# The gated output bias of the first attention: added to the residual by GpSimd, four tiles at a time, or by a TensorE product of ones and three bf16 parts

## The chip, the cores and the metric

One core of one Trainium2 chip runs the whole program. Times are device microseconds (us) of that core; lower is better. The engines are called by the names that the profile has for them: PE is TensorE (PEld its weight loads), DVE VectorE, ACT ScalarE, POOL GpSimd, SP SyncE.

## What is computed

Two layers work on 8192 tokens of 128 numbers (128 sequences of 64). The change lies in the first step of the first layer, an attention over a context, whose result is gated and added to x:

```python
def _L0_xattn_ref(q_in, k_in, v_in, mask, Wq, bq, Wk, bk, Wv, bv, Wo, bo):
    q = _split_heads(q_in @ Wq + bq)              # 16 heads of 8
    k = _split_heads(k_in @ Wk + bk)
    v = _split_heads(v_in @ Wv + bv)
    logits = jnp.einsum('bhqd,bhkd->bhqk', q, k) / jnp.sqrt(jnp.asarray(D_QKV, jnp.float32))
    w = jax.nn.softmax(logits - mask * FMAX, axis=-1)
    o = jnp.einsum('bhqk,bhkd->bhqd', w, v)
    return o.transpose(0, 2, 1, 3).reshape(...) @ Wo + bo

x = x + jnp.tanh(g_xattn[0]) * _L0_xattn_ref(_layernorm(x, axis=-1), ctx_1024, ctx_1024, mask, ...)
x = x + jnp.tanh(g_ffn[0]) * _L0_ffn_ref(_layernorm(x, axis=-1), ...)    # 8 experts, top 2
x = x + jnp.tanh(g_xattn[1]) * _L1_xattn_ref(_layernorm(x, axis=-1), ctx_1024, ctx_1024, mask_BxS2_bk1, ...)
x = x + jnp.tanh(g_ffn[1]) * _L1_ffn_ref(_layernorm(x, axis=-1), ...)
```

With the gate written as g = tanh(g_xattn[0]), the first line adds o @ (g Wo) + g bo to x. It is where g bo is added that differs.

## The kernel before

x lies in SBUF for the whole run, as 64 tiles of 128 tokens by 128 numbers (`x_sb`). The first attention runs over these tiles in 64 steps plus three that drain it; t is the step, s = t // 4 the quad (four tiles, `QUAD`), j = t % 4 the place in it. Each engine has its own queue, written out by hand in the order of the steps, and waits on semaphores. The routing of the tokens to experts (logits, first and second choice, places, scattering of rows by indirect DMA) is woven into the same steps some tiles later, and so are the keys and values of the second attention.

What a step t holds, for each engine, in the order of its queue:

- PE: scores of two tiles (even j, L798); `heads_product(t)`: 32 small products of probabilities and values for tile t-3 (L897), and behind them, for tile t-4, the output product into `turn`, a strip of the PSUM bank `ps_o` (L903 and L904), whose end is told by `o_ps`; `probs_transposes(t)` of tile t-2 (L913, waits for POOL's `shifted`); some projections; `heads_transpose(t)` (L922), which writes `turn` again and so waits for DVE's `y_sb` (the residual has been read out) and `o_sb`.
- DVE: scores minus mask (L1390); `reciprocals` (L1363) and `head_sums` (L1367), which wait for `o_ps`; `residual(t)` (L1373), x_sb plus `turn` for tile t-4; `x_stats` (L1377); routing steps, above all `places(c)` at j = 2 of every even s from 4 on (L1208 to L1217); and the row maximum `top` (L1425), the last large thing of the step.
- POOL: scores minus `top` in place (L500, semaphore `shifted`), then at some steps small things, and from step 18 on two indirect DMAs that scatter rows (`send_rows`, L481). At j = 0 it also takes the powers of the second layernorm (L454, L456).
- ACT: exponentials of the transposed scores (L618), the copy of the heads (L622), normalised x and others.

The gated bias `bo` (scaled by tanh at L398) is put into PSUM by PE: `bias_parts()` on POOL splits it once, at t = 1, into three bf16 parts in rows 0, 32 and 64 of `bias_row` (`bias_step` counts to 9), and in each of the 64 steps a product of `ones_row` and `bias_row` starts the accumulation in `turn` (L903) that the fp32 product of heads and `wo` ends (L904).

Of the kernel before, what the change touches and what calls it, by code (L numbers as in the profile page):

```python
# [5 lines left out]
ALU = mybir.AluOpType  # L6
ACT = mybir.ActivationFunctionType
AX_X = mybir.AxisListType.X
F32 = mybir.dt.float32
F32R = mybir.dt.float32r  # L10
BF16 = mybir.dt.bfloat16
# [3 lines left out]
P = 128  # L15
BATCH, SEQ, DM = 128, 64, 128
NTOK = BATCH * SEQ
TILES = NTOK // P
QUAD = 4
# [39 lines left out]
def layer0_and_experts(nc, ctx, d, g, sb, sem):  # L59

    x_sb, stats, ident, tg = g["x_sb"], g["stats"], g["ident"], g["tanh_gates"]
# [4 lines left out]
    wq, wk, wv, wo, bv, bo = (sb(f"a_{n}", [P, DM], F32) for n in ("wq", "wk", "wv", "wo", "bv", "bo"))  # L66
    bq, bk = (sb(f"a_{n}", [P, 1], F32) for n in ("bq", "bk"))
    mask = sb("a_mask", [P, SEQ], F32)
    with ExitStack() as until_routed:
        def first(name, shape, dt):  # L70
# [21 lines left out]
    xn_t, ctx_t, heads_t = g["keys0"], g["values0"], g["wq1"]  # L92
# [6 lines left out]
    probs_t = sb("a_probs_t", [P, 2, GROUPS, P], F32)  # L99
    rsum = sb("a_rsum", [P, HEADS], F32)  # L100
    heads = sb("a_heads", [P, HEADS, DH], F32)
    bias_hi, bias_mid, bias_row, ones_row = (sb(f"a_{n}", [65, P], BF16) for n in ("bias_hi", "bias_mid", "bias_row", "ones_row"))
    bias_rest = sb("a_bias_rest", [65, P], F32)

    TE = [P, CT, EXPERTS]
    rw = sb("r_rw", [EXPERTS, DM], F32)
# [47 lines left out]
    (gates_in, q_in, k_in, v_in, mask_in, wo_in, ident_step, gates_ready, bq_set, own_set, stats1, step1, var_ready,  # L154
     rstd_ready, nmr_ready, vals_set, ones_set, mask_set, bo_set, xn_ready, xt_ps, ct_ps, xt_sb, ct_sb, q_ps,
     k_ps, q_sb, k_sb, v_ps, v_sb, s_ps, s_sb, top_ready, shifted, pt_ps, pt_sb, o_ps, rsum_ready, o_sb, ot_ps, ot_sb,
     y_sb, stats2, bias_step) = (sem("a_" + n) for n in (
         "gates_in", "q_in", "k_in", "v_in", "mask_in", "wo_in", "ident_step", "gates_ready", "bq_set", "own_set", "stats1", "step1",
         "var_ready", "rstd_ready", "nmr_ready", "vals_set", "ones_set", "mask_set", "bo_set", "xn_ready",
         "xt_ps", "ct_ps", "xt_sb", "ct_sb", "q_ps", "k_ps", "q_sb", "k_sb", "v_ps", "v_sb", "s_ps", "s_sb",  # L160
         "top_ready", "shifted", "pt_ps", "pt_sb", "o_ps", "rsum_ready", "o_sb", "ot_ps", "ot_sb", "y_sb", "stats2", "bias_step"))
    (rw_in, bias_in, consts, const_step, resets_set, mv_ready, var2_ready, rstd2_ready, nmr2_ready, row_ready, x2t_ps, x2t_sb, l_ps,
     l_sb, small_ps, small_sb, hi_done, lo_done, weights_out, first_pick, second_pick, ratio_ready, cn_ps, placed, gate_set,
     ids, ends_ready, table_step, tables_ready, padded) = (sem("r_" + n) for n in (
# [25 lines left out]
    turn = ps_o[:, TURN_AT:TURN_AT + P]  # L190
# [177 lines left out]
    def _(pool):  # L368
# [30 lines left out]
        pool.tensor_scalar(wo[:], wo[:], tg[:, 0:1], None, ALU.mult).then_inc(bo_set, 1)  # L399
        pool.wait_ge(bo_set, 2)  # L400

        def bias_parts():
            pool.memset(ones_row[:], 1.0).then_inc(bias_step, 1)
            pool.memset(bias_row[:], 0.0).then_inc(bias_step, 1)
            pool.tensor_copy(bias_hi[:], bo[0:65]).then_inc(bias_step, 1)
            pool.wait_ge(bias_step, 3)
            pool.tensor_tensor(bias_rest[:], bo[0:65], bias_hi[:], ALU.subtract).then_inc(bias_step, 1)
            pool.wait_ge(bias_step, 4)
            pool.tensor_copy(bias_mid[:], bias_rest[:]).then_inc(bias_step, 1)
            pool.wait_ge(bias_step, 5)  # L410
            pool.tensor_tensor(bias_rest[:], bias_rest[:], bias_mid[:], ALU.subtract).then_inc(bias_step, 1)
            pool.wait_ge(bias_step, 6)
            pool.tensor_copy(bias_row[0:1], bias_hi[0:1]).then_inc(bias_step, 1)
            pool.wait_ge(bias_step, 7)
            pool.tensor_copy(bias_row[32:33], bias_mid[32:33]).then_inc(bias_step, 1)
            pool.wait_ge(bias_step, 8)
            pool.tensor_copy(bias_row[64:65], bias_rest[64:65]).then_inc(bias_step, 1)
            pool.wait_ge(bias_step, 9)

        def routing_consts(nth):  # L420

# [73 lines left out]
        for s in range(SUPERS):  # L495
            for j in range(QUAD):
                t = s * QUAD + j
                m = s - 2
                pool.wait_ge(top_ready, t + 1)
                pool.tensor_tensor(probs[:, j], probs[:, j], top[:, j].unsqueeze(2).broadcast_to([P, HEADS, SEQ]),  # L500
                                   ALU.subtract).then_inc(shifted, 1)
                if j == 0 and m >= 0:
                    powers(m)
                if t == 1:
                    bias_parts()
                r = 2 + s
                if j == 2 and there(r, len(ROUNDS)):
                    pool.wait_ge(var_ready, r + 1)
                    scale(ROUNDS[r][0] // QUAD)
                if j == 3 and there(r, len(ROUNDS)):  # L510
                    for n in range(ROUNDS[r][0] // QUAD + 1, ROUNDS[r][1] // QUAD):
                        scale(n)
                if s == 1:
                    routing_consts(j)
                c = s // 2 - 1
                if j == 0 and s % 2 == 0 and RING <= c < NCH:
                    renumber(c)
                if t >= SCATTER_LAG:
                    send_rows(t - SCATTER_LAG)
# [271 lines left out]
    def _(pe):  # L791
# [97 lines left out]
        def heads_product(t):  # L889
            j = t % QUAD  # L890
# [8 lines left out]
                                       vals[(t - 3) // QUAD % 2][:, (j + 1) % 4, b, cols], start=True, stop=True)  # L899
            if there(t - 4, TILES):  # L900
                if t == 4:
                    pe.wait_ge(bias_step, 9)
                pe.matmul(turn, ones_row[:], bias_row[:], start=True, stop=False)  # L903
                mm = pe.matmul(turn, heads_t[:], wo[:], start=False, stop=True)  # L904
            mm.then_inc(o_ps, 1)

        def probs_transposes(t):
# [22 lines left out]
        for s in range(SUPERS):  # L930
            n, u, m = s + 1, s % 2, s - 2
            for j in range(QUAD):
                t = s * QUAD + j
# [190 lines left out]
    def _(dve):  # L1124
# [244 lines left out]

        def residual(t):  # L1370
            dve.wait_ge(o_ps, t - 2)
            xs = x_sb[:, t - 4]
            dve.tensor_tensor(xs, xs, turn, ALU.add).then_inc(y_sb, 1)  # L1373

# [1015 lines left out]
```

## Time and profile before

| | |
|---|---|
| median of 3 runs | 895.19 us (894.82 to 900.1) |
| span of the profiled execution | 960.7 us |
| busy in it: PE, DVE, ACT, POOL | 746.5, 742.0, 612.7, 594.2 us |
| first attention | from about 15 us to about 415 us of the span |

The profiled execution was 65 us longer than the median of the runs that were timed. A row of the timeline gives the start, the duration, the engine, the line, the operation, what is written from what is read, and how many instructions were put together; in brackets stands the idle time before it and who ended it. In a row of waits stand the waiting engine and line, the releaser, the total in us, the number of waits and the longest. Ends of matmuls are modelled, so that starts on PE are the better measure of its pace.

### The profile page before, as it was taken

The numbers are of one execution on the slowest core, as the hardware profiler recorded it, in microseconds if no ns is written. First come the engines' busy times: TensorE is split into PE (matmuls) and PEld (weight loads), VectorE is DVE, ScalarE is ACT, GpSimd is POOL, SyncE is SP. The second block draws the span as 40 slices with busy tenths as digits, with TensorE's granted clock in tenths as the row PEclk, the third lists the DMA queues.
The fourth block names the chain that finished last, engine by engine and source line by source line (L and its number), as shares of the span: only waits on it lengthen the run. The fifth ranks groups of instructions, "written<-read, shape, count | busy, mean of one in ns | idle before, by whom it ended". The sixth has DMA issues, their size and how long they took to land. (4 is left out here: it accounts for less than half of the span.)

```text
span 960.7 us, 19492 instructions
## 1 busy us (share of the span) xinstructions
PE 746.5 (78%) x6609; PEld 573.8 (60%) x6612; DVE 742.0 (77%) x1800; ACT 612.7 (64%) x1222; POOL 594.2 (62%) x571
## 2 busy tenths in 40 slices
PE   4898788988888888788698888999963889256255
PEld 2666577666666667666576766777751667122144
DVE  5999987877777887568566666777844799799998
ACT  5666556757576664567366656666753878399493
POOL 4675377777777777564556566665665983388600
PEclk9999989999999999899798999999985999676556
DMA  9327222222223123646476566575627832000023
GB/s 246 101 78 128 86 73 101 82 101 78 100 80 111 47 93 123 214 140 204 150 260 217 193 239 216 208 259 202 222 93 239 273 110 78 14 0 1 0 66 111
DMA packets 88625, 128.20 MB, mean 133 GB/s; under 512 B 19392, under 2 KB 62352, under 8 KB 82512
## 3 DMA queue, kind: packets, MB, share of 16 engines
q1 hardware_dynamic: 78528, 107.63, 34.6%
q0 software_dynamic: 9120, 18.91, 5.6%
q8 instruction: 54, 0.88, 0.4%
q10 hardware_dynamic: 880, 0.43, 0.2%
q14 instruction: 43, 0.35, 0.1%
HBM read 82.66 MB, written 44.18 MB: 132 GB/s over the span
## 5 line engine op out<-in xcount | busy, mean ns | idle before, releaser
L491 POOL DMA_INDIRECT m_results<-a_probs,e_to x156 | 161.6, 1036 | 94.5 <-issue 50.2
L500 POOL TENSOR_TENSOR a_probs<-a_probs,a_top 128x1024 f32<-128x1024 f32 x64 | 122.0, 1907 | 91.5 <-DVE a_top L1425 90.6
L481 POOL DMA_INDIRECT m_tokens_to<-r_rows,r_place x128 | 131.3, 1026 | 53.3 <-issue 31.0
L710 ACT ACTIVATE room<-a_ps_s,e_bias 128x512 f32<-128x512 f32 x156 | 107.3, 697 | 79.5 <-PE a_ps_s L1007 64.6
L1452 DVE CAST e_hp<-room 128x512 fp32r<-128x512 f32 x156 | 70.1, 449 | 82.8 <-ACT room L710 30.9
L618 ACT ACTIVATE a_probs_t<-a_ps_pt 128x512 f32<-128x512 f32 x128 | 70.1, 592 | 94.3 <-PE a_ps_pt L913 91.2
L1454 DVE TENSOR_TENSOR e_hp<-room,e_hp 128x512 fp32r<-128x512 f32 x156 | 109.9, 705 | 5.4
L1390 DVE TENSOR_TENSOR a_probs<-a_ps_s,a_mask 128x1024 f32<-128x1024 f32 x64 | 77.9, 1217 | 16.0 <-PE a_ps_s L798 11.5
L897 PEld LDWEIGHTS a_ps_o<-a_vals,a_probs_t 128*64 128x64 f32 x2048 | 68.1, 140 | 26.0 <-issue 25.2
L897 PE MATMUL a_ps_o<-a_vals,a_probs_t 128*64 128x18 f32 x2048 | 75.7, 214 | 4.8 <-issue 4.6
L1425 DVE TENSOR_REDUCE a_top<-a_probs 128x16 f32<-128x1024 f32 x64 | 77.2, 1206 | 0.2
L913 PE MATMUL a_ps_pt<-ident,a_probs 128*128 128x128 f32 x512 | 73.5, 291 | 1.5 <-DVE n_values L1287 1.2
L1003 PE MATMUL a_ps_s<-e_xt,e_weights 128*128 128x512 f32 x156 | 68.2, 437 | 8.2 <-issue 5.1
L2219 DVE TENSOR_REDUCE d_hpeak<-d_hid 128x1 f32<-128x2048 f32 (+1 forms) x36 | 70.6, 2043 | 3.4 <-ACT d_hid L2116 3.4
L913 PEld LDWEIGHTS a_ps_pt<-ident,a_probs 128*128 128x128 f32 x512 | 63.7, 151 | 2.9 <-DVE n_values L1287 2.4
L1007 PE MATMUL a_ps_s<-e_xt,e_weights 128*128 128x512 f32 x156 | 62.6, 401 | 0.0
L1004 PE MATMUL a_ps_s<-e_xt,e_weights 128*128 128x512 f32 x156 | 62.5, 401 | 0.0
L1014 PE MATMUL a_ps_pt<-e_hp,e_weights 128*128 128x512 f32 x100 | 41.5, 415 | 12.1 <-ACT room L722 7.9
L1363 DVE RECIPROCAL a_rsum<-a_ps_o 128x16 f32<-128x16 f32 x64 | 16.1, 251 | 41.5 <-PE a_ps_o L904 23.3
L729 ACT ACTIVATE a_probs<-a_ps_pt,room 128x128 f32<-128x128 f32 x156 | 44.2, 373 | 3.1 <-PE a_ps_pt L1032 3.1
L922 PE MATMUL a_ps_o<-ident,a_heads 128*128 128x128 f32 x64 | 20.8, 325 | 32.1 <-DVE x_sb L1373 30.1
L553 ACT ACTIVATE room<-a_ps,a_own_bk,a_own 128x512 f32<-128x512 f32 x64 | 44.6, 783 | 1.8 <-PE a_ps L818 1.8
(334 smaller groups left out, 2012.9 us busy)
## 6 DMA issues: line engine op xcount, KB each, us to landing
e_weights<-m_weights_to SPq DMA_DIRECT2D x39, 1024.0 KB
room<-m_tokens_to SPq DMA_DIRECT2D x39, 264.0 KB
m_weights_to<-r_parts SPq DMA_DIRECT2D x8, 1024.0 KB
c_two<-m_results SPq DMA_DIRECT2D x3, 1536.0 KB, 11.8
a_ctx_in<-in_ctx_dram SPq DMA_DIRECT2D x17, 256.0 KB, 3.5
m_keys_t<-n_keys SPq DMA_DIRECT2D x16, 256.0 KB
m_values<-n_values SPq DMA_DIRECT2D x16, 256.0 KB
out_dram<-x_sb SPq DMA_DIRECT2D x15, 256.0 KB, 2.3
```

The source lines that it names most:

```text
L481: pool.indirect_dma_start(tokens_to, bass.IndirectOffsetOnAxis(ap=place[:, k, q:q + 1], axis=0), rows[:, c % RING, q % CT, k, :], None).th ...
L491: pool.indirect_dma_start(results, bass.IndirectOffsetOnAxis(ap=to[:, v, r:r + 1], axis=0), y[:, v, r], None).then_inc(returned[v], 16)
L500: pool.tensor_tensor(probs[:, j], probs[:, j], top[:, j].unsqueeze(2).broadcast_to([P, HEADS, SEQ]), ALU.subtract).then_inc(shifted, 1)
L618: act.activation(probs_t[:, j % 2, 4 * h:4 * h + 4, :], ps_pt[h][:], ACT.Exp).then_inc(pt_sb, 1)
L710: act.activation(h[:, c], ps_h[c], ACT.Gelu_apprx_tanh, bias=bias[:, n % ROWS, c:c + 1]).then_inc(h_sb, 1)
L897: mm = pe.matmul(ps_o[SEQ * b:SEQ * b + SEQ, cols], probs_t[:, (j + 1) % 2, gr, SEQ * b:SEQ * b + SEQ], vals[(t - 3) // QUAD % 2][:, (j + ...
L913: mm = pe.transpose(ps_pt[h][:, k, :], probs[:, (t + 2) % 4, 8 * h + 2 * k:8 * h + 2 * k + 2] .rearrange("p j k -> p (j k)"), ident[:])
L1390: dve.tensor_tensor(probs[:, j].rearrange("p (i k) q -> p i k q", i=BANDS), ps_s[:, :, j % 2], mask[:].unsqueeze(1).unsqueeze(1).broadcast ...
L1425: dve.tensor_reduce(top[:, j], probs[:, j], AX_X, ALU.max).then_inc(top_ready, 1)
L1452: dve.tensor_copy(hp[:, c, 0], h[:, c]).then_inc(h_hi, 1)
L1454: dve.tensor_tensor(hp[:, c, 1], h[:, c], hp[:, c, 0].bitcast(F32), ALU.subtract).then_inc(h_lo, 1)
L2219: dve.tensor_reduce(hpeak[:, e, column:column + 1], h, AX_X, op).then_inc(hpeak_ready, 1)
```

## The change

POOL no longer splits the bias. In its place, at j = 1 of each of the 16 quads and right behind that step's subtraction, it adds `bo` to the quad's four tiles of `x_sb` in one 128x512 instruction (`add_bias`). It waits for `xn_ready`, that is until ACT has normalised these four tiles, since the layernorm must see x without the bias. PE's product of ones and bias parts goes away, in all 64 steps; the output product starts its own accumulation, and at t = 4 waits for the gated `wo` (`bo_set`) in place of the nine steps of the split. DVE's residual waits for `bias_added` of its quad as well. Five small tiles in SBUF go away.

```diff
@@ gpsimd
-        def bias_parts():
-            pool.memset(ones_row[:], 1.0).then_inc(bias_step, 1)
-            pool.memset(bias_row[:], 0.0).then_inc(bias_step, 1)
-            pool.tensor_copy(bias_hi[:], bo[0:65]).then_inc(bias_step, 1)
...
-            pool.tensor_copy(bias_row[64:65], bias_rest[64:65]).then_inc(bias_step, 1)
-            pool.wait_ge(bias_step, 9)
+        def add_bias(n):
+            four = slice(QUAD * n, QUAD * n + QUAD)
+            pool.wait_ge(xn_ready, QUAD * n + QUAD)
+            pool.tensor_tensor(x_sb[:, four], x_sb[:, four], bo[:].unsqueeze(1).broadcast_to([P, QUAD, DM]), ALU.add)\
+                .then_inc(bias_added, 1)
...
-                if t == 1:
-                    bias_parts()
+                if j == 1:
+                    add_bias(s)
@@ tensor
                 if t == 4:
-                    pe.wait_ge(bias_step, 9)
-                pe.matmul(turn, ones_row[:], bias_row[:], start=True, stop=False)
-                mm = pe.matmul(turn, heads_t[:], wo[:], start=False, stop=True)
+                    pe.wait_ge(bo_set, 2)
+                mm = pe.matmul(turn, heads_t[:], wo[:], start=True, stop=True)
@@ vector
         def residual(t):
             dve.wait_ge(o_ps, t - 2)
+            dve.wait_ge(bias_added, (t - 4) // QUAD + 1)
             xs = x_sb[:, t - 4]
             dve.tensor_tensor(xs, xs, turn, ALU.add).then_inc(y_sb, 1)
```

The order of PE's instructions in one step of the first attention before (L897 the heads, L903 the bias, L904 the output product, L913 the transposes of the scores, L922 the transpose of the heads):

```order
L897 MATMUL a_ps_o<-a_vals,a_probs_t 64x18 [waits a_v_sb,a_y_sb,a_pt_sb,a_ot_sb,a_o_sb]
L897 MATMUL a_ps_o<-a_vals,a_probs_t 64x18 x15
L903 MATMUL a_ps_o<-a_bias_row,a_ones_row 128x128
L904 MATMUL a_ps_o<-a_wo,wq 128x128
L913 MATMUL a_ps_pt<-ident,a_probs 128x128 [waits a_pt_sb,a_shifted,a_xt_sb]
L913 MATMUL a_ps_pt<-ident,a_probs 128x128 x7
```

The same of a step in the changed kernel, where the lines are L883, L889, L898 and L907:

```order
L883 MATMUL a_ps_o<-a_vals,a_probs_t 64x18 [waits a_v_sb,a_y_sb,a_pt_sb,a_ot_sb,a_o_sb]
L883 MATMUL a_ps_o<-a_vals,a_probs_t 64x18 x15
L889 MATMUL a_ps_o<-a_wo,wq 128x128
L898 MATMUL a_ps_pt<-ident,a_probs 128x128 [waits a_pt_sb,a_shifted,n_v1_raw]
L898 MATMUL a_ps_pt<-ident,a_probs 128x128 x7
L907 MATMUL a_ps_o<-ident,a_heads 128x128 [waits a_o_sb,a_y_sb]
```

The one bf16 product between the heads and the output product is gone, and nothing else has moved on PE.

The order of POOL's instructions at the last quad of the changed kernel (L486 is the subtraction that was L500, L440 and L442 are the powers, L467 the scatter that was L481):

```order
L486 TENSOR_TENSOR a_probs<-a_probs,a_top 128x1024 [waits a_top_ready]
L440 TENSOR_TENSOR r_rstd<-r_mv,r_power 128x4 [waits r_mv_ready]
L442 TENSOR_TENSOR r_rstd<-r_rstd,r_power 128x4 [waits r_var2_ready]
L467 DMA m_tokens_to<-r_rows,r_place 73216x132 x2
L486 TENSOR_TENSOR a_probs<-a_probs,a_top 128x1024 [waits a_top_ready]
L403 TENSOR_TENSOR x_sb<-x_sb,a_bo 128x512 [waits a_xn_ready]
L467 DMA m_tokens_to<-r_rows,r_place 73216x132 x2
L486 TENSOR_TENSOR a_probs<-a_probs,a_top 128x1024 [waits a_top_ready]
```

L403 is the new instruction: behind the subtraction of j = 1 and ahead of that step's two scatters; before, the scatters followed at once.

## Rows read from the trace of the kernel before

**Rows 1.** Busy time by stage: span, then PE, PEld, DVE, ACT, POOL, clock, DMA
```profile
15.00:400.00 385.00, 326.70 (x4429) 255.79 (x4428) 315.85 (x841) 236.07 (x475) 261.30 (x232) 0.96 0.34 106
```

**Rows 2.** Waits between 60 and 400 us: total, times, longest
```profile
POOL a_probs L500 <- DVE a_top L1425: 78.9, 28, 4.7
...
PE a_ps_o L922 <- DVE x_sb L1373: 25.5, 27, 2.3
DVE a_rsum L1363 <- PE a_ps_o L904: 23.3, 18, 2.8
```

**Rows 3.** All instructions of line L903: min/median/max ns, first and last start
```profile
L903 PE MATMUL a_ps_o<-a_bias_row,a_ones_row x64: 229/230/289, 34.5 to 413.2; 65*128 65x128 bf16 x64
```

**Rows 4.** Timeline of PE and DVE, steps 39 and 41
```profile
240.54 0.23 PE L903 MATMUL a_ps_o<-a_bias_row,a_ones_row 65*128 65x128 bf16 x1
240.60 0.44 PE L904 MATMUL a_ps_o<-a_wo,wq 128*128 128x128 f32 x2
240.88 1.04 PE L913 MATMUL a_ps_pt<-ident,a_probs 128*128 128x128 f32 x8
...
241.13 0.26 DVE L1363 RECIPROCAL a_rsum<-a_ps_o 128x16 f32<-128x16 f32 x1 [1.23 <-PE a_ps_o L904]
...
253.11 1.04 PE L913 MATMUL a_ps_pt<-ident,a_probs 128*128 128x128 f32 x8
```

**Rows 5.** POOL's groups of instructions: count, busy us, mean ns, idle before
```profile
L2072 POOL TENSOR_TENSOR x_sb<-x_sb,room 128x512 f32<-128x512 f32 x16 | 20.0, 1271 | 0.0
...
L2059 POOL TENSOR_TENSOR room<-x_sb,mean 128x512 f32<-128x512 f32 x16 | 16.8, 1051 | 25.4 <-DVE ext L2190 24.4 <-DVE room L2211 0.9
```

**Rows 6.** Timeline of POOL, the first and last of the nine split instructions
```profile
24.33 0.20 POOL L403 MEMSET a_ones_row<- 65x128 bf16 x1
...
27.03 0.29 POOL L417 CAST a_bias_row<-a_bias_rest 1x128 bf16<-1x128 f32 x1
```

**Rows 7.** Timeline of POOL, a quad of odd s (steps 37 to 40)
```profile
236.11 1.91 POOL L500 TENSOR_TENSOR a_probs<-a_probs,a_top 128x1024 f32<-128x1024 f32 x1
...
244.81 1.92 POOL L500 TENSOR_TENSOR a_probs<-a_probs,a_top 128x1024 f32<-128x1024 f32 x1
...
253.50 1.90 POOL L500 TENSOR_TENSOR a_probs<-a_probs,a_top 128x1024 f32<-128x1024 f32 x1 [4.37 <-DVE a_top L1425]
```

**Rows 8.** Timeline, DVE's variances beside and without POOL's subtraction
```profile
27.88 1.90 POOL L500 TENSOR_TENSOR a_probs<-a_probs,a_top 128x1024 f32<-128x1024 f32 x1 [0.56 <-DVE a_top L1425]
...
28.54 1.27 DVE L1136 TENSOR_TENSOR mean<-stats 128x12 f32<-128x12 f32 x1
...
49.94 0.18 DVE L1136 TENSOR_TENSOR mean<-stats 128x12 f32<-128x12 f32 x1
```

**Rows 9.** Timeline of POOL and DVE, a quad of even s (s = 14)
```profile
354.45 1.92 POOL L500 TENSOR_TENSOR a_probs<-a_probs,a_top 128x1024 f32<-128x1024 f32 x1
...
357.03 0.29 DVE L1208 TENSOR_TENSOR_SCAN r_upto<-r_resets,r_total 128x72 f32<-128x72 f32 x1
...
360.35 1.90 POOL L500 TENSOR_TENSOR a_probs<-a_probs,a_top 128x1024 f32<-128x1024 f32 x1 [1.49 <-DVE a_top L1425]
```

**Rows 10.** Timeline of POOL, DVE and PE, s = 13 (steps 53 to 55)
```profile
332.01 1.91 POOL L500 TENSOR_TENSOR a_probs<-a_probs,a_top 128x1024 f32<-128x1024 f32 x1
...
334.00 0.27 DVE L1315 TENSOR_TENSOR r_past<-r_tnum,r_tile_end 128x104 f32<-128x104 f32 x1
...
338.42 0.28 DVE L1373 TENSOR_TENSOR x_sb<-x_sb,a_ps_o 128x128 f32<-128x128 f32 x1
...
338.75 0.33 PE L922 MATMUL a_ps_o<-ident,a_heads 128*128 128x128 f32 x1
```

**Rows 11.** Timeline of DVE and PE, the residual and L922 in step 59
```profile
362.15 0.28 DVE L1373 TENSOR_TENSOR x_sb<-x_sb,a_ps_o 128x128 f32<-128x128 f32 x1
...
363.22 0.27 PE L922 MATMUL a_ps_o<-ident,a_heads 128*128 128x128 f32 x1
```

**Rows 12.** Timeline of POOL, its first wait behind the last quad
```profile
396.27 0.19 POOL L454 TENSOR_TENSOR r_rstd<-r_mv,r_power 128x4 f32<-128x4 f32 x1 [5.05 <-DVE r_mv L1357]
```

More of the change, by code:

```diff
@@ L101, in layer0_and_experts @@
     heads = sb("a_heads", [P, HEADS, DH], F32)
-    bias_hi, bias_mid, bias_row, ones_row = (sb(f"a_{n}", [65, P], BF16) for n in ("bias_hi", "bias_mid", "bias_row", "ones_row"))
-    bias_rest = sb("a_bias_rest", [65, P], F32)
     TE = [P, CT, EXPERTS]
@@ L156, in layer0_and_experts @@
      k_ps, q_sb, k_sb, v_ps, v_sb, s_ps, s_sb, top_ready, shifted, pt_ps, pt_sb, o_ps, rsum_ready, o_sb, ot_ps, ot_sb,
-     y_sb, stats2, bias_step) = (sem("a_" + n) for n in (
+     y_sb, stats2, bias_added) = (sem("a_" + n) for n in (
          "gates_in", "q_in", "k_in", "v_in", "mask_in", "wo_in", "ident_step", "gates_ready", "bq_set", "own_set", "stats1", "step1",
@@ L160, in layer0_and_experts @@
          "xt_ps", "ct_ps", "xt_sb", "ct_sb", "q_ps", "k_ps", "q_sb", "k_sb", "v_ps", "v_sb", "s_ps", "s_sb",
-         "top_ready", "shifted", "pt_ps", "pt_sb", "o_ps", "rsum_ready", "o_sb", "ot_ps", "ot_sb", "y_sb", "stats2", "bias_step"))
+         "top_ready", "shifted", "pt_ps", "pt_sb", "o_ps", "rsum_ready", "o_sb", "ot_ps", "ot_sb", "y_sb", "stats2", "bias_added"))
     (rw_in, bias_in, consts, const_step, resets_set, mv_ready, var2_ready, rstd2_ready, nmr2_ready, row_ready, x2t_ps, x2t_sb, l_ps,
@@ L400, in _ @@
         pool.wait_ge(bo_set, 2)
-        def bias_parts():
-            pool.memset(ones_row[:], 1.0).then_inc(bias_step, 1)
-            pool.memset(bias_row[:], 0.0).then_inc(bias_step, 1)
-            pool.tensor_copy(bias_hi[:], bo[0:65]).then_inc(bias_step, 1)
[L406 to L416, printed above, removed]
-            pool.tensor_copy(bias_row[64:65], bias_rest[64:65]).then_inc(bias_step, 1)
-            pool.wait_ge(bias_step, 9)
+        def add_bias(n):
[3 more added lines that the diff above has]
+                .then_inc(bias_added, 1)
         def routing_consts(nth):
```

## The prediction

> **What bounds the kernel now.** I read the busy time by stage first. Over the first attention PE is busy 326.7 of 385.0 us, DVE 315.9, POOL 261.3, ACT 236.1, with the clock at 0.96 of the higher level (2.4 GHz) [rows 1]. No engine is full, so the 64 steps (385.0 / 64 = 6.0 us each) are set by a ring of waits, and the waits come next. Between 60 and 400 us, 57 steps, PE waits 27 times for DVE's residual before it may transpose the heads, DVE waits 18 times for the output product, and POOL waits 28 times, 78.9 us in all, for DVE's row maximum [rows 2]. So the ring runs PE, DVE, PE: heads and output product, reciprocal to residual, transpose of the heads. POOL hangs on it as a side branch with time to spare. The change takes a little from PE inside the ring and puts more on POOL beside it. The reader should ask three things: how wide PE's slot is, whether POOL can take the addition, and whom a longer POOL disturbs.
>
> **PE, 64 bf16 products removed.** One lasts 0.230 us by its own row [rows 3]. That is not what it costs, since matmuls overlap: in the timeline L903 starts at 240.54 and L904 at 240.60 [rows 4]. The 64 distances from L903 to L904 lie between 0.06 and 0.08 us, so I take 0.065: 64 x 0.065 = 4.2 us of PE's time. It shortens the run only where the ring passes through PE. For the floor I count the steps in which DVE waits for the output: 18 of 57 [rows 2], so 4.2 x 18 / 57 = 1.3 us. For the ceiling I take every step, 4.2. Beside those 18 there are steps in which PE goes into L922 without any wait (about 57 - 27 = 30, partly the same ones), where PE itself is the pace. I choose 40 slots of 64, between the two ends: **-2.6 us**.
>
> **POOL, the split removed, 16 additions put in.** The split ran from 24.33 to 27.32, 3.0 us once [rows 6]. It was wanted by PE at step 4, at 34.5 us [rows 3], so it cost nothing and its going gives nothing. For an addition the trace has the same shape in the last stage: 128x512, x_sb plus a bias repeated four times, 1.271 us; the nearest cheaper row, where the second input is one number for each tile, is 1.051 [rows 5]. I take 1.27; between 1.05 and 1.27 the total is 16.8 to 20.3 us. Who covers it: POOL's steps of a quad are a subtraction of 1.9 us each and two scatters ((244.81 - 236.11) / 2 = 4.35 us from one subtraction to the next [rows 7], so some 2.45 for the two), and the tightest place is a quad of odd s. There the three subtractions from j = 1 on run back to back with the scatters, the first at 236.11 and the last at 244.81, and then POOL idles 4.37 us until DVE's maximum releases it at 253.50 [rows 7]. The addition comes behind the first of these and moves the other two by 1.27. The last of them would end at 246.73 + 1.27 = 248.00, while PE transposes that tile at 253.11 [rows 4], 5.1 us later. The subtraction of j = 1 itself, which has the least room (ended 238.02, used by PE at 240.88 [rows 4], 2.86 us), lies ahead of the addition and is not moved. In quads of even s POOL idles 1.49 us (s = 14) or more before the next subtraction and takes up the 1.27 there [rows 9]; only at s = 13 is the idle shorter, 0.59, and the rest of the 1.27 is then at most 0.7 us of lateness. Behind the last quad POOL idles 5.05 us until 396.27 [rows 12], so the scatters that follow are not pushed either. Term: **0**; without that cover it would be 20.3 - 3.0 = 17.3.
>
> **The new waits.** DVE's residual of quad n comes first in step 4n + 4; the addition was issued behind the subtraction of step 4n + 1, three steps of 6 us earlier. ACT has normalised quad n in the quad before, so POOL does not stand at `xn_ready`, with its scatters queued behind it. Both are 0.
>
> **DVE, held up by POOL's addition.** This is the term that speaks against the change. Beside POOL's subtraction a DVE instruction of 128x12 whose two inputs both lie in SBUF took 1.27 us, from 28.54 to the very end of the subtraction at 29.78, and 0.18 without it [rows 8]. DVE's large instructions of the stage (PSUM and one SBUF input, or one input) show no such stretch. So I looked which two-input instructions of DVE fall into the 1.27 us behind the subtraction of j = 1. Of `places`, L1208 starts at 357.03, 0.66 us behind the subtraction's end at 356.37 [rows 9], and would be held to 357.60. The same is seen in s = 6, 8, 10, 12 and 14, with distances of 0.79, 0.78, 0.91, 0.68 and 0.66 us, which makes 0.44 + 0.45 + 0.32 + 0.55 + 0.57 = 2.3 us. In s = 13 the table look-up starts at 334.00, just as the subtraction (332.01 + 1.91) is over [rows 10], and would lose 1.2 us. In the other ten quads nothing falls in. What of this reaches the ring is read one step later, where PE transposes the heads: in step 55 the residual ends at 338.70 and PE goes at 338.75, no room [rows 10]; in step 59 it ends at 362.43 and PE goes at 363.22, 0.7 us of room [rows 11]. Steps 35 and 43 look like 59, and steps 27 and 51 like 55. So s = 6, 12 and 13 pay, 0.44 + 0.55 + 1.15 = **+2.1 us**; bounds are 0 (DVE's wait of the next step takes it up) and 3.5.
>
> The Trainium skill, SBUF — State Buffer, section "Who interferes with whom", says that a DVE instruction with two SBUF inputs and a GpSimd one that reads SBUF lock each other out for the whole instruction; this trace agrees, 1.27 against 0.18 us. The Trainium skill's GPSIMD Engine Reference, section "Engine selection", advises VectorE for elementwise additions, and section "Elementwise — side-by-side cycle accounting" gives 4497 ns for 2048 numbers per partition, which makes an estimate of 1.12 us for 512 and 18.0 us for 16, where the row makes 20.3; POOL's idle time covers either.
>
> **The sum.** -2.6 + 0 + 2.1 = -0.5 us on a span of 960.7, so 960.2. The profiled execution is 65 us above the median of the timed runs, 895.19; carried over in proportion the change is again -0.5: 894.7.
>
> **Rivals.** (a) *Likeliest, 0.83:* slots gained and lock losses nearly cancel. With its bounds, -4.2 + 0 to -1.3 + 3.5 = +2.2, it gives 891 to 897.5. (b) *Slower by the lock, 0.06:* if the additions move relative to DVE's work so that a two-input instruction is held the whole 1.27 us in every quad and nothing takes it up, 16 x 1.27 - 4.2 = +16.1, 911.3. It decides (more than 9 us) from about 10 quads on; against it stand ten quads in which nothing falls into the window. (c) *Slower by POOL's load, 0.04:* in the timed runs the steps are shorter than 6.0 us, by the ratio of the times 5.6. If POOL's idle time is what shrank, the later subtractions reach PE late and up to 17.3 us come back, 912.5. Against it: 78.9 us of idle POOL over 57 steps, 1.4 us in each, 5.5 a quad, and 1.27 is needed. (d) *Faster, 0.07:* the bf16 product between fp32 ones costs its full 0.230 us, in every step: 64 x 0.23 = -14.7, 880.5. Against it is the 0.06 us between starts, and DVE's reciprocal at 241.13, 0.09 us behind the modelled end of the output product (240.60 + 0.44) [rows 4], so that PE's records hide no more time at that place.
>
> About 1% (9 us) is what can be told from no change for this kernel, since its own runs lie between 894.82 and 900.1. That gives faster 0.07, same 0.83, slower 0.10. The range must hold (a) and the scatter of the runs, of which one was 5 us above the median: 889 to 901.
>
> **What would show it.** In the changed profile: 64 fewer matmuls, with the first output matmul starting about 0.03 us behind the last one of the heads. 16 POOL additions of 1.27 us. The subtraction of odd quads' j = 2 starting some 3 us behind DVE's maximum, instead of 1.7, with no wait of PE for it. No wait of DVE's residual for POOL. L1208's successor lasting 0.6 to 0.9 us instead of 0.29 in five quads. The last step of the attention within 3 us of where it was (L903 last at 413.2 [rows 3]). A residual that waits for `bias_added`, PE waiting for `shifted`, or stretched DVE instructions in most quads would make it wrong.

## The result, and the profile after

The changed kernel takes **911.76 us** (median of 4, 910.37 to 918.22) beside 896.28 us (median of 4, 894.82 to 900.1) of the kernel before: ratio 1.0169, 95% interval 1.0117 to 1.022. It is 15 us slower. The forecast was 894.7, range 889 to 901, with 0.10 for slower.

The profiled execution of the changed kernel (busy us, share of its span, instructions):

```profile
span 907.4 us, 19437 instructions
...
PE 732.0 (81%) x6548; PEld 560.3 (62%) x6548; DVE 755.6 (83%) x1800; ACT 618.6 (68%) x1222; POOL 608.9 (67%) x578
```

This span is 53 us *below* the 960.7 of the trace that the prediction was read from, although the kernel is slower. The two profiled executions cannot be compared as they are, and the experiments have to settle that first. Waits of the changed kernel between 60 and 400 us (total, times, longest):

```profile
POOL a_probs L486 <- DVE a_top L1411: 53.5, 29, 3.9
...
PE a_ps_o L907 <- DVE x_sb L1359: 27.4, 28, 2.3
DVE a_rsum L1348 <- PE a_ps_o L889: 26.6, 21, 4.4
```

POOL's wait for the row maximum fell from 78.9 to 53.5 us; the other two were 25.5 and 23.3 [rows 2] and seem hardly to have moved. Against a trace of the kernel before that belongs to the timed runs (below) the reading is another: POOL's wait was 57.9 there, and PE's for the residual 19.1. PE waits nowhere for `shifted`, no residual waits for POOL, the addition lasts 1.27 us as forecast. What is new stands where DVE's scan of `places` (L1193, before L1208) meets POOL, here in s = 8:

```profile
213.93 1.92 POOL L486 TENSOR_TENSOR a_probs<-a_probs,a_top 128x1024 f32<-128x1024 f32 x1
215.79 1.28 POOL L403 TENSOR_TENSOR x_sb<-x_sb,a_bo 128x512 f32<-128x512 f32 x1
...
215.95 1.30 DVE L1193 TENSOR_TENSOR_SCAN r_upto<-r_resets,r_total 128x72 f32<-128x72 f32 x1
```

In the trace before it lasted 0.29 us and began 0.66 us behind the subtraction's end in s = 14 [rows 9], 0.78 us in s = 8. Here, in s = 8, it begins 0.10 us behind it (215.85) and ends at 217.25, 0.18 us behind the end of the addition (217.07).

### The profile page after: what moved, and what is told of

Its sections match the earlier page's. It is cut to its first block and busy times, and to the rows that moved or that the text cites. A ratio compares the mean times of both kernels' runs of the same rounds, so it can differ in the third digit from the quotient of the medians.

```text
span 907.4 us, 19437 instructions
## 1 busy us (share of the span) xinstructions
PE 732.0 (81%) x6548; PEld 560.3 (62%) x6548; DVE 755.6 (83%) x1800; ACT 618.6 (68%) x1222; POOL 608.9 (67%) x578
## 5 line engine op out<-in xcount | busy, mean ns | idle before, releaser
L477 POOL DMA_INDIRECT m_results<-a_probs,e_to x156 | 158.1, 1014 | 58.7 <-issue 36.4
L486 POOL TENSOR_TENSOR a_probs<-a_probs,a_top 128x1024 f32<-128x1024 f32 x64 | 122.1, 1907 | 69.4 <-DVE a_top L1411 68.8
L467 POOL DMA_INDIRECT m_tokens_to<-r_rows,r_place x128 | 132.6, 1036 | 47.8 <-issue 31.2
L1438 DVE CAST e_hp<-room 128x512 fp32r<-128x512 f32 x156 | 73.1, 469 | 39.2 <-ACT room L696 34.5
L883 PEld LDWEIGHTS a_ps_o<-a_vals,a_probs_t 128*64 128x64 f32 x2048 | 66.7, 141 | 20.3 <-issue 19.7
L883 PE MATMUL a_ps_o<-a_vals,a_probs_t 128*64 128x18 f32 x2048 | 73.1, 214 | 0.3 <-ACT wq L608 0.3
L898 PE MATMUL a_ps_pt<-ident,a_probs 128*128 128x128 f32 x512 | 70.7, 284 | 1.5 <-DVE n_values L1272 1.5
L988 PE MATMUL a_ps_s<-e_xt,e_weights 128*128 128x512 f32 x156 | 66.5, 426 | 5.6 <-DMA e_weights<-m_weights_to 5.6
L898 PEld LDWEIGHTS a_ps_pt<-ident,a_probs 128*128 128x128 f32 x512 | 60.8, 147 | 3.2 <-DVE n_values L1272 2.0
L992 PE MATMUL a_ps_s<-e_xt,e_weights 128*128 128x512 f32 x156 | 61.4, 394 | 0.0
L989 PE MATMUL a_ps_s<-e_xt,e_weights 128*128 128x512 f32 x156 | 61.3, 393 | 0.0
L2102 ACT ACTIVATE d_hid<-d_ps_h,d_b,d_outscale 128x512 f32<-128x512 f32 x64 | 44.7, 788 | 1.5 <-PE d_ps_h L2143 1.5
L907 PE MATMUL a_ps_o<-ident,a_heads 128*128 128x128 f32 x64 | 20.7, 324 | 29.8 <-DVE x_sb L1359 28.8
L2143 PE MATMUL d_ps_h<-d_xqt,d_wqt 128*128 128x512 bf16 x64 | 26.8, 566 | 21.7 <-ACT d_xqt L2094 21.7
```

What stands on the lines that cost most here:

```text
L467: pool.indirect_dma_start(tokens_to, bass.IndirectOffsetOnAxis(ap=place[:, k, q:q + 1], axis=0), rows[:, c % RING, q % CT, k, :], None).th ...
L477: pool.indirect_dma_start(results, bass.IndirectOffsetOnAxis(ap=to[:, v, r:r + 1], axis=0), y[:, v, r], None).then_inc(returned[v], 16)
L883: mm = pe.matmul(ps_o[SEQ * b:SEQ * b + SEQ, cols], probs_t[:, (j + 1) % 2, gr, SEQ * b:SEQ * b + SEQ], vals[(t - 3) // QUAD % 2][:, (j + ...
L898: mm = pe.transpose(ps_pt[h][:, k, :], probs[:, (t + 2) % 4, 8 * h + 2 * k:8 * h + 2 * k + 2] .rearrange("p j k -> p (j k)"), ident[:])
L1438: dve.tensor_copy(hp[:, c, 0], h[:, c]).then_inc(h_hi, 1)
```

## Experiments

Every ratio is to the kernel before, timed beside it on the same chip. For the traces I use one measure, the distance from one row maximum of DVE (`top`) to the next, which is the length of a step of the first attention.

**The two kernels once more on one chip.** The same source as before and as after, no edit.

> The kernel before, profiled once more, because its profiled execution (960.7 us) lay 65 us above its timed runs while that of the changed kernel (907.4) did not. All theories: 895 to 900 us timed. If the first profile was a disturbed execution, this one's span is near 893, and the waits of the two attention traces can be compared; if profiling itself costs this kernel 65 us, the span is again near 960.

> The changed kernel, a second time and on the same chip as the others: 911 us if the 1.7 per cent hold on another chip, 896 if they were scatter.

On this chip the kernel before takes 960.07 us (median of 31, 948 to 971), 7% more than in the timing above. `base_again` measured 1.0015 (0.997 to 1.006), `after_again` 1.0057 (1.0004 to 1.011). The span of the first profile, 960.7, fits this chip's 960 and not the 895 that the prediction was to be made for. So the trace I had read was, as far as its numbers tell, of such a chip, on which this kernel runs slower (below: the slow chip). There the change costs little. The same two kernels on other chips:

> The changed kernel on whatever chip comes next. In the group before, all four kernels and the kernel before lay at 958 to 962 us, where the kernel before had 896 in the first comparison: chips differ by more than the change. Theory A (the loss of 15 us is real where the expert stage isn't slowed by its loads): 1.01 to 1.02 times the kernel before on a chip on which that takes 895 us, 1.00 on one where it takes 960. Theory C (the loss was the scatter of single executions, 948 to 971 for one kernel on one chip): 1.00 on both.

> The kernel before, for a trace from a chip on which it takes some 897 us: the first two traces of it are from chips on which it takes 960. On such a chip the distances between DVE's row maxima in steps 26, 34, 42, 50, 54 and 58 should be those of the kernel without the bias (6.0, 6.0, 6.3, 6.2, 5.9 and 6.2 us), and the 64 maxima take 344 us from first to last, 4 us less without PE's product if that product costs its slot.

On the first of them before took 897.82 us (median of 13) and the changed kernel 915.25 (median of only 4, 905.22 to 919.55): 1.0179 (1.0109 to 1.025). `base_fast`, the kernel before on a third chip, took 896.65 with a span of 894.8 (one run). This profile fits the timed runs; from here on it is the comparison. Its waits between 60 and 400 us:

```profile
POOL a_probs L500 <- DVE a_top L1425: 57.9, 29, 5.2
...
DVE a_rsum L1363 <- PE a_ps_o L904: 23.9, 20, 5.8
...
PE a_ps_o L922 <- DVE x_sb L1373: 19.1, 24, 2.1
```

Beside these, PE's wait for DVE's residual has grown from 19.1 to 27.4 us in the changed kernel. The loss stands in the ring itself, at the place where PE waits for DVE, and not at POOL.

What differs between the chips in the place in question: PE, DVE and POOL of the kernel before in the first trace, s = 8 (in brackets the idle time before):

```profile
209.64 0.91 PE L897 MATMUL a_ps_o<-a_vals,a_probs_t 128*64 128x18 f32 x15
210.96 0.31 PE L897 MATMUL a_ps_o<-a_vals,a_probs_t 128*64 128x18 f32 x4 [0.41 <-issue]
211.71 0.58 PE L897 MATMUL a_ps_o<-a_vals,a_probs_t 128*64 128x18 f32 x13 [0.44 <-issue]
...
211.28 1.91 POOL L500 TENSOR_TENSOR a_probs<-a_probs,a_top 128x1024 f32<-128x1024 f32 x1
...
211.81 1.22 DVE L1390 TENSOR_TENSOR a_probs<-a_ps_s,a_mask 128x1024 f32<-128x1024 f32 x1 [0.93 <-remote]
...
213.97 0.29 DVE L1208 TENSOR_TENSOR_SCAN r_upto<-r_resets,r_total 128x72 f32<-128x72 f32 x1
```

and the same stretch in `base_fast`:

```profile
208.13 1.11 PE L897 MATMUL a_ps_o<-a_vals,a_probs_t 128*64 128x18 f32 x32
...
209.29 1.21 DVE L1390 TENSOR_TENSOR a_probs<-a_ps_s,a_mask 128x1024 f32<-128x1024 f32 x1
...
209.77 1.91 POOL L500 TENSOR_TENSOR a_probs<-a_probs,a_top 128x1024 f32<-128x1024 f32 x1
...
211.38 0.47 DVE L1208 TENSOR_TENSOR_SCAN r_upto<-r_resets,r_total 128x72 f32<-128x72 f32 x1
211.88 0.17 DVE L1211 COPY r_total<-r_upto 128x8 f32<-128x8 f32 x1
```

On the slow chip both engines stand still for some 0.9 us ahead of the scan, which no engine of the core explains, so that DVE came to it 0.78 us *behind* the subtraction (211.28 + 1.91 = 213.19). (`base_again` shows the same: 0.87 us without work, then the scan 0.67 us behind the subtraction.) On the other chip they don't stand still, and DVE comes to it 0.30 us *before* the subtraction's end (211.68), and is already held: 0.47 us in place of 0.29, ending at 211.85. In s = 6, 10, 12 and 14 it comes 0.29 to 0.54 us before the end. An addition put right behind the subtraction then finds the scan waiting; only in s = 8, where the changed kernel's step 33 is longer, does it come 0.1 us behind the end.

**The product of ones and bias gone, nothing on POOL.** The changed kernel without the addition and without DVE's wait for it; the bias is left out of the result.

```diff
-                if j == 1:
-                    add_bias(s)
...
-            dve.wait_ge(bias_added, (t - 4) // QUAD + 1)
```

> The changed kernel without the 16 additions and without DVE's wait for them: the bias is left out of the computation. PE's product is gone, and nothing stands in its place. Theory A (POOL's additions cost the time, by DVE's lock or by POOL's load): 891 to 895 us, the -2.6 us of the forecast. Theory B (taking PE's product away costs it, by a lower clock or by a shifted order of waits): 908 to 912.

> The changed kernel without the additions (the bias is left out of the computation), beside it. Theory A with POOL's additions as the cause: 0.995 to 1.00 times the kernel before on a fast chip. Theory B (PE's missing product is the cause): as slow as the changed kernel. Theory C: 1.00 like all.

1.002 (0.9974 to 1.0067) on the slow chip, 1.0015 (0.9979 to 1.0052) on the other. Taking 64 products from PE gives back nothing that the timing can show, at most 0.2%. The trace says how little there is; PE in a step of `base_fast`:

```profile
278.05 1.11 PE L897 MATMUL a_ps_o<-a_vals,a_probs_t 128*64 128x18 f32 x32
279.10 0.23 PE L903 MATMUL a_ps_o<-a_bias_row,a_ones_row 65*128 65x128 bf16 x1
279.16 0.44 PE L904 MATMUL a_ps_o<-a_wo,wq 128*128 128x128 f32 x2
279.44 0.82 PE L913 MATMUL a_ps_pt<-ident,a_probs 128*128 128x128 f32 x6
```

and in one of the changed kernel (the trace shown first):

```profile
217.87 1.11 PE L883 MATMUL a_ps_o<-a_vals,a_probs_t 128*64 128x18 f32 x32
218.91 0.49 PE L889 MATMUL a_ps_o<-a_wo,wq 128*128 128x128 f32 x2
219.23 1.04 PE L898 MATMUL a_ps_pt<-ident,a_probs 128*128 128x128 f32 x8
```

From the start of the heads to the output product it is 1.11 us before and 1.04 after (medians over more than 50 steps each): the slot of 0.065 did go. But the output product then takes from its start to the transposes' 0.32 to 0.33 in place of 0.27 to 0.28, and from heads to transposes 1.37 stands against 1.39. What is left is 0.02 us a step, 1.3 us in 64. And since the output product's two passes now last 0.49 us and not 0.44, its modelled end moved from 1.55 to 1.53 us behind the heads' start, 0.02 again. Why the passes take longer the trace doesn't say.

**The addition alone, the product kept.** The kernel before with the 16 additions at the same place, counted on `bias_step`; the bias is added twice.

```diff
...
+                if j == 1:
+                    add_bias(s)
...
+            dve.wait_ge(bias_step, 9 + (t - 4) // QUAD + 1)
```

> The kernel before with the 16 additions put in beside PE's product, so that the bias is added twice. Theory A: 911 to 915 us, as slow as the changed kernel or 3 us slower. Theory B: 895 to 898, since PE has all its work still. If both are slow only together (neither this nor the run without bias is slow), the sum of small shifts is the cause.

> The kernel before with the 16 additions put in and PE's product kept (the bias is added twice), now with traces of both kinds of chip in mind: 1.015 to 1.02 on a chip where the kernel before takes 897 us, since the additions alone make the loss; 1.00 where it takes 960.

1.0029 (0.9984 to 1.0075) on the slow chip, 1.0161 (1.0109 to 1.0213) on another, against 1.017 to 1.018 for the changed kernel. Within the intervals the whole of the loss comes with the additions.

**The addition moved away from the scan.** At j = 2 from s = 5 on, behind another subtraction.

```diff
-                if j == 1:
+                if j == (1 if s < 5 else 2):
```

> The changed kernel with the additions of quads 5 to 15 behind the subtraction of j = 2 in place of j = 1, where DVE has no instruction with two SBUF inputs for the next 3 us. POOL's load is the same. Theory L (POOL's addition holds up DVE's scan, L1193, for its whole length in six quads and L1297 in one): the 1.2 us in steps 26, 34, 42, 50, 54 and 58 are gone, 1.003 to 1.008 times the kernel before where the changed one has 1.018. Theory P (POOL's 20 us of added load, whatever its place): 1.015 to 1.020.

1.0066 (1.0033 to 1.0099), 903.53 us beside the 912.38 of the kernel above on the same chip: more than half of the loss is gone, with as many additions of the same kind.

**The same time on POOL without reading SBUF.** In place of each addition, at its old place, three writes of zeros into an unused tile; the bias is left out.

```diff
-            pool.tensor_tensor(x_sb[:, four], x_sb[:, four], bo[:].unsqueeze(1).broadcast_to([P, QUAD, DM]), ALU.add)\
-                .then_inc(bias_added, 1)
+            for k in range(3):
+                if 3 * n + k:
+                    pool.wait_ge(bias_added, 3 * n + k)
+                pool.memset(dummy[:], 0.0).then_inc(bias_added, 1)
...
-            dve.wait_ge(bias_added, (t - 4) // QUAD + 1)
+            dve.wait_ge(bias_added, 3 * ((t - 4) // QUAD + 1))
```

> The changed kernel with three memsets of 128x380 in place of each addition, some 1.3 us of POOL at the same place that write SBUF and read nothing (the bias is left out of the computation). Theory L by reads: DVE's scan isn't held beyond the subtraction's end (0.5 us), and the time is that of the kernel without bias, 1.000 to 1.005. Theory P: 1.015 to 1.020, as the changed kernel. If the scan is held though nothing is read, the lock is of writes too, and the time is that of the changed kernel as well.

1.0066 (1.0036 to 1.0096), above the 1.000 to 1.005 that was expected if only reads hold DVE. POOL's group of these writes, and its timeline at s = 8 (the three writes as one row, then the second of them by itself):

```profile
L407 POOL MEMSET a_dummy<- 128x380 f32 x48 | 20.0, 417 | 1.8
```

```profile
205.85 1.92 POOL L489 TENSOR_TENSOR a_probs<-a_probs,a_top 128x1024 f32<-128x1024 f32 x1
207.69 1.38 POOL L407 MEMSET a_dummy<- 128x380 f32 x3
208.18 0.41 POOL L407 MEMSET a_dummy<- 128x380 f32 x1
...
207.86 0.29 DVE L1196 TENSOR_TENSOR_SCAN r_upto<-r_resets,r_total 128x72 f32<-128x72 f32 x1
208.19 0.44 DVE L1199 COPY r_total<-r_upto 128x8 f32<-128x8 f32 x1
```

POOL is as busy as with the additions (20.0 against 16 x 1.27 = 20.3 us) and at the same place, and the scan runs in 0.29 us beside it. In s = 6, 10, 12 and 14, where the subtraction already holds it, the scan is over 0.18 us behind the subtraction, while the writes go on. So it is the reading that holds the scan, not POOL's time. But the small copy behind the scan, which has one input, lasts 0.44 us in place of 0.17 and ends at 208.63, 0.04 us behind the second write: some instructions of DVE are held by writes. The scan over the whole run, minimum, median and maximum in ns, in `base_fast`, the changed kernel, the addition with the product kept, the later addition and the write-only one:

```profile
L1208 DVE TENSOR_TENSOR_SCAN r_upto<-r_resets,r_total x8: 287/470/719, 123.1 to 425.4; 128x72 f32<-128x72 f32 x8
```

```profile
L1193 DVE TENSOR_TENSOR_SCAN r_upto<-r_resets,r_total x8: 285/1496/1953, 120.9 to 435.1; 128x72 f32<-128x72 f32 x8
```

```profile
L1216 DVE TENSOR_TENSOR_SCAN r_upto<-r_resets,r_total x8: 291/1502/1945, 121.2 to 433.1; 128x72 f32<-128x72 f32 x8
```

```profile
L1193 DVE TENSOR_TENSOR_SCAN r_upto<-r_resets,r_total x8: 287/392/735, 118.9 to 427.3; 128x72 f32<-128x72 f32 x8
```

```profile
L1196 DVE TENSOR_TENSOR_SCAN r_upto<-r_resets,r_total x8: 287/390/727, 119.3 to 423.7; 128x72 f32<-128x72 f32 x8
```

The Trainium skill, SBUF — State Buffer, section "Who interferes with whom", states just this border: a DVE instruction with two SBUF inputs contends with a GpSimd one that reads SBUF, not with one that only writes it. By that rule, the traces agree: 1.30 us beside the addition, 0.29 beside the writes.

**A version without either loss.** The additions spread by hand to steps in which neither a scan nor the layernorm's powers stand behind them (for s from 6 on mostly steps of the quads of odd s).

```diff
+        ADDS = {1: (0,), 4: (1,), 9: (2,), 13: (3,), 17: (4,), 22: (5,), 23: (6,), 30: (7,), 31: (8,), 38: (9,), 39: (10,),
+                46: (11,), 47: (12,), 55: (13, 14), 62: (15,)}
...
-                if j == 1:
-                    add_bias(s)
+                for n in ADDS.get(t, ()):
+                    add_bias(n)
```

> The changed kernel with every addition in a step where POOL has idle time and DVE no two-input instruction behind POOL's subtraction: steps 1, 4, 9, 13, 17, and from quad 5 on two additions in each odd quad (steps 22 and 23, 30 and 31, 38 and 39, 46 and 47, both 13 and 14 in step 55, 15 in step 62). Theory L with the rest of the loss (1.007 of the later placing against 1.0015 without bias) made of POOL's powers coming late to DVE and ACT in quads 1, 13 and 15: 1.000 to 1.004 times the kernel before. If the rest is POOL's load wherever it stands: 1.006 to 1.010. A gain over the kernel before isn't expected by either, since PE's product gave back nothing. On a chip where the kernel before takes 960 us: 1.00 by both.

900.75 us beside 898.49, 1.0031 (1.0006 to 1.0057). This is the change nearly without its cost, and it still isn't faster than the kernel before, as the 1.0015 without any addition already says: no run shows a gain on PE.

**The steps side by side.** Length of a step in us (from one row maximum to the next), all on the chips where the kernel before takes some 897 us; below, all 63 of them.

| step | before (`base_fast`) | no addition | later | write only | product kept | spread | after |
|---|---|---|---|---|---|---|---|
| 26 (s = 6, scan) | 6.02 | 6.03 | 6.03 | 6.06 | 7.24 | 6.03 | 7.23 |
| 34 (s = 8, scan) | 6.02 | 6.03 | 5.84 | 6.02 | 6.88 | 5.84 | 6.85 |
| 42 (s = 10, scan) | 6.27 | 6.29 | 6.29 | 6.32 | 7.50 | 6.28 | 7.50 |
| 50 (s = 12, scan) | 6.19 | 6.22 | 6.21 | 6.24 | 7.43 | 6.19 | 7.42 |
| 54 (s = 13, scan of the tiles' ends) | 5.93 | 5.94 | 5.95 | 5.89 | 7.16 | 5.94 | 7.16 |
| 58 (s = 14, scan) | 6.21 | 6.21 | 6.21 | 6.24 | 7.44 | 6.21 | 7.42 |
| 33 | 4.89 | 4.90 | 5.20 | 5.20 | 5.19 | 5.20 | 5.20 |
| 44 | 6.67 | 6.65 | 6.65 | 6.64 | 6.65 | 6.64 | 7.98 |
| 7 and 8 | 12.15 | 10.63 | 11.87 | 11.91 | 11.85 | 10.64 | 11.00 |
| 18 and 20 | 13.77 | 13.25 | 16.53 | 14.00 | 13.86 | 15.45 | 15.66 |
| 61 | 4.56 | 4.56 | 5.80 | 4.56 | 4.56 | 4.56 | 4.57 |
| all 63 | 348.2 | 343.9 | 350.9 | 346.7 | 355.5 | 346.4 | 360.0 |

The six steps in which a scan runs grow by 1.21 + 0.83 + 1.23 + 1.23 + 1.23 + 1.21 = **6.9 us**, in the two kernels with the addition ahead of the scan and in no other of the table. That is the lock, paid in full in five of them; in s = 8 it is 0.83 us.

Step 44 is 1.3 us longer in the changed kernel. PE there waits longer for DVE's late residual and then runs slow. PE between the maxima of steps 43 and 44, in the second trace of the changed kernel (`after_third`):

```profile
262.29 0.33 PE L907 MATMUL a_ps_o<-ident,a_heads 128*128 128x128 f32 x1 [1.55 <-DVE x_sb L1359]
263.52 1.09 PE L856 MATMUL a_ps_pt<-ident,r_rows 128*128 128x128 f32 x4 [0.90 <-issue]
264.53 2.01 PE L784 MATMUL a_ps_s<-room 32*64 32x256 f32 x32
```

and the stretch in the same kernel (span; busy of PE, PEld, DVE, ACT, POOL; granted clock, 1.00 being 2.4 GHz):

```profile
263.00:267.00 4.00, 3.48 (x41) 2.12 (x41) 2.50 (x6) 2.29 (x5) 3.51 (x4) 0.57 0.23 79
```

In `base_fast` PE waited 0.30 us there, the granted clock stayed at 1.00, and the same two groups took 0.63 and 1.12 us. The sequence is the held scan, a late residual, an idle PE and then PE at the lower of its two levels, 1.2 GHz, for some us. The kernel with the product kept has the held scan and, at the same place, a wait of 1.53 us, yet its two groups took 0.63 and 1.12 us and its step 44 is 6.65. So the wait alone does not decide it, and what tips it stays open; the 1.3 us stand in both traces of the changed kernel from such chips.

Steps 7 and 8 are 10.6 us where POOL has no addition or write at step 5 and 11.9 where it has. This is the lock once more, by an instruction that only writes. The addition pushes a large write of POOL's, which clears `r_pad`, back by 1.3 us, into DVE's variances. The write and the first held instruction, which has one SBUF input, in `after_third`, and that instruction in the spread kernel, free:

```profile
48.21 3.62 POOL L413 MEMSET r_pad<- 128x4224 f32 x1
...
50.65 1.21 DVE L1125 TENSOR_SCALAR mean<-mean 128x12 f32<-128x12 f32 x1
```

```profile
52.11 0.17 DVE L1128 TENSOR_SCALAR mean<-mean 128x12 f32<-128x12 f32 x1
```

It ends at 51.86, 0.03 us behind the write; in `e4_memset` it is the same, 1.28 us. The three instructions just ahead of it (L1121 to L1123, two SBUF inputs each) run beside the same write in 0.17 to 0.18 us. In step 8 an instruction with two inputs (L1137) is held to the end of POOL's later subtraction, 0.67 us in place of 0.30.

`base_fast` and the changed kernel's first trace show other values in steps 6 to 8; their granted clock from 32 to 44 us is 0.93 and 0.92, that of the other columns 1.00, and in step 7 of `base_fast` POOL's subtraction holds L1136 for 1.90 us. This matters for the last row. The 63 steps are 4.3 us shorter without the product and the addition, about what 64 slots would give; but 4.0 of them are at steps 2, 6, 7 and 18, which the kernel before has in the short form as well in its first trace (5.32, 4.54, 4.94, 6.61 us). In most other steps the two columns differ by 0.00 to 0.03 us.

Step 33 is 0.3 us longer in every kernel with additions or writes, the spread one too; I have no reason for it. In the later placing steps 55 and 61 pay. In step 55 the addition holds a conversion of DVE's with one SBUF input, 1.26 us in place of 0.15:

```profile
325.62 1.28 POOL L403 TENSOR_TENSOR x_sb<-x_sb,a_bo 128x512 f32<-128x512 f32 x1
...
325.68 1.26 DVE L1320 CAST tables<-r_texp 1x13 uint32<-1x13 f32 x1
```

(step 56 gives 0.7 us of it back). Ahead of step 61 POOL's powers come late to DVE, which waits 2.51 us for them in place of 1.28. In step 58 the lock had worked the other way round: POOL's addition lasted 2.32 us, beside a DVE instruction of 128x1024 with two inputs (L1278, 1.21 us) that had begun 0.01 us earlier.

So the 1.0066 of the writes against the 1.0015 without anything on POOL is not the price of POOL's time alone. A part of it is DVE held by writes, and the two intervals overlap a little (1.0036 to 1.0096, 0.9979 to 1.0052).

## Why the prediction was wrong

**PE, -2.6 us: 0.** The row of 0.065 us between the starts was right, and the slot went, but I took the distance to the next start for what its removal gives. The output product took most of it back: 0.02 us a step is left, and the timed kernel without product and addition shows 1.0015 (0.9979 to 1.0052), no gain; 2.6 us would be 0.9971. The rule "a shorter start-to-start distance is a shorter step" is the failed half of this term; the choice of 40 slots never mattered.

**POOL's load, 0: nearly right.** 16 x 1.27 was right to the hundredth, no subtraction reached PE late, no residual waited. What I had not counted is that the addition moves POOL's other work against DVE's: the large write at step 7 (with step 8 1.2 us) and the 0.3 us at step 33, together about 1.5 us in the traces and, by the write-only runs (1.0066 - 1.0015), about 0.5% or 4 us in time. I had looked only at the subtractions as what the addition could make late, and only at DVE instructions with two SBUF inputs as what could be held.

**The new waits, 0: right.**

**The lock, +2.1 us: the step that failed.** The mechanism was read rightly, down to the quads (s = 6, 8, 10, 12, 14 and the table of s = 13) and the price of s = 13 (1.15, measured 1.23). The other five were mis-sized: 0.32 to 0.57 us each, of which I let two pay, 0.44 + 0.55, against five that paid, 0.83 to 1.23 us each. In place of 2.1 us the lock cost 6.9 us in these six steps.

In s = 13 the number was right for an instruction that was not the one. The look-up that I named stayed at 0.27 us; what was held is the scan ahead of it, in the trace before and in the changed kernel:

```profile
333.47 0.49 DVE L1312 TENSOR_TENSOR_SCAN r_tile_end<-r_one,r_ntile 128x8 f32<-128x8 f32 x1
```

```profile
329.69 1.71 DVE L1297 TENSOR_TENSOR_SCAN r_tile_end<-r_one,r_ntile 128x8 f32<-128x8 f32 x1
```

It ended at 333.96 before, 0.04 us behind the subtraction (332.01 + 1.91 [rows 10]): it was already held there. Of the six places it was the only one at which the first trace shows the instruction already waiting.

The sizes of the five came from distances of 0.66 to 0.91 us between the subtraction's end and the scan, and these distances were those of a chip on which DVE stands still ahead of the scan. On that chip the arithmetic holds; `after_again`, s = 14, POOL and DVE:

```profile
359.62 1.91 POOL L486 TENSOR_TENSOR a_probs<-a_probs,a_top 128x1024 f32<-128x1024 f32 x1
361.48 1.27 POOL L403 TENSOR_TENSOR x_sb<-x_sb,a_bo 128x512 f32<-128x512 f32 x1
```

```profile
362.12 0.80 DVE L1193 TENSOR_TENSOR_SCAN r_upto<-r_resets,r_total 128x72 f32<-128x72 f32 x1
```

0.80 us where "0.6 to 0.9 us instead of 0.29" was forecast, and in the five quads 0.65 to 0.80. On the chips where before takes 897 us the scan arrives before the subtraction is over, or 0.1 us behind it, and what holds it is then not a part of the addition, but nearly the whole.

**Carrying the sum over, "in proportion".** This is where the first mistake lay. The 65 us between the profile and the timed runs were in the prediction twice, and I took them for a uniform stretch. They are not one. DVE's waits of the kernel before between 60 and 400 us that no engine of the core releases are 18.0 + 4.2 = 22.2 us in the first trace and absent in `base_fast`:

```profile
DVE a_rsum L1363 <- remote: 18.0, 5, 6.3
...
DVE a_probs L1390 <- remote: 4.2, 4, 1.2
```

and the stage from 400 to 650 us (span; busy of PE, PEld, DVE, ACT, POOL; clock; DMA share; GB/s) moved less in the first trace, the upper row, than in `base_fast`, the lower:

```profile
400.00:650.00 250.00, 215.08 (x1038) 171.91 (x1037) 169.19 (x366) 154.81 (x316) 152.63 (x150) 0.95 0.58 202
```

```profile
400.00:650.00 250.00, 240.28 (x1188) 196.55 (x1187) 202.03 (x415) 186.04 (x375) 176.39 (x174) 0.99 0.70 243
```

The distance of the scan from the subtraction's end did not scale; it changed its sign (0.78 us behind, 0.30 before, in s = 8).

**The rivals.** (b) named the right mechanism, and its 911.3 us is nearly the measured 911.76; but it reached its 16.1 us with 16 quads of 1.27, less 4.2 from PE, where six steps pay and PE gives nothing. That the numbers agree is chance. It was said to decide from ten quads on; six made 6.9 us, and with what hangs on them and without PE's 4.2 us on the other side the loss was clear. (c) was put at POOL's subtractions and did not come about there. (d) is refuted: nothing is gained where the product alone is taken out, where 14.7 us would be 0.984.

**What the traces place of the loss.** The timed loss is 15.1 us (0.0169 x 896.28). Moving the additions from the scan takes back 1.0 to 1.1% of the kernel's time, some 9 to 10 us; the traces place 6.9 us at the six steps and 1.3 at step 44. Leaving the additions out gives 0.5% more.

The changed kernel's trace is 11.7 us longer than `base_fast` over the 63 steps and 12.6 at the end. It holds about 5 us at steps 20 to 23, with PE at a granted clock of 0.50 to 0.62 from 133.5 to 145.6 us. These I don't count as the change's: step 20 has a long form, 8.8 to 9.9 us, in traces of the kernel before (9.13 in the first, 6.66 in `base_again`) and of the kernel without addition (9.53 in `e1_no_bias`, 6.64 in `e1_no_bias_b`) as well as after (9.04, 6.65 in `after_again`). In the seven traces with the long form PE had waited 2.11 to 2.33 us for the residual of the step, in the others at most 1.50. But of the 5 us 2.6 are at steps 21 and 22, and these are so long in this one trace only.

Between 3 and 5 us of the timed loss so stay without a place. A single trace can't give it one: from the last maximum to the end of the span it is 528.3 us in `base_fast`, 529.5 and 529.0 in the changed kernel's two traces, 532.5 with the product kept and 537.8 in `e1_no_bias_b`, although nearly the same work stands there in all of them. Open too is what makes the chips differ. On the slow chip the lock's 0.4 to 0.5 us in five quads and 1.2 in one, some 3.5 us, are 0.4% of 960 and lie within the 1.0057 (1.0004 to 1.011) measured there.

## What to carry to other kernels

When the profiled execution is some per cent away from the timed runs, find out in which rows it differs before reading distances of tenths of a us from it, and price a lock between DVE and POOL with the DVE instruction arriving at the worst moment, not where the trace has it. Put a POOL instruction that reads SBUF only behind work of POOL at which DVE has no instruction with two SBUF inputs waiting. One that only writes spares these, but not DVE's copies, conversions and operations with a constant, which have one input and were held as well (from 0.17 to 1.21 us beside the write of `r_pad`); look for both kinds, and also at what else of POOL's the new instruction pushes back. And before counting the removal of an overlapped matmul as a gain, take the distance over its neighbours and not to the next start: 64 slots of 0.065 us were worth nothing that could be measured here.

## What the runs showed that was not expected

- A DVE instruction held by one POOL instruction was not let in between it and the next. In five of the six places in `after_third` the scan was already waiting 0.30 to 0.55 us ahead of the subtraction's end, and it stayed held through the addition as well. That of s = 10 lasted 1.95 us and ended 0.18 us behind the addition; in all six places it ended 0.05 to 0.18 us behind it. With writes or a scatter in the addition's place the waiting scan ended 0.04 to 0.18 us behind the subtraction.
- A write-only POOL instruction does not hold the scan (0.29 us), but it holds some DVE instructions with one SBUF input: the small copy took 0.44 us beside it and 0.17 without, the operation with a constant at step 7 took 1.21 us and 0.17.
- The same kernel takes 960 us on one chip and 896 to 898 on the others. A change can be worth 1.7% on one kind and 0.6% or less on the other.
- In the changed kernel a wait of 1.55 us on PE in place of 0.30 was followed by some 4 us at a mean granted clock of 0.57, and a loss of 1.2 us in one step by 1.3 in the next but one; with the product kept, a wait of 1.53 us was not.
